# The last stage of a one-core transformer kernel: a written-out pass order, six shared PSUM banks, and the second bias through DRAM

## The chip, the cores and the metric

The kernel runs on one core of a Trainium2 chip. The metric is the device time of one execution in microseconds (us). The core has five engines with a queue of instructions each: PE (TensorE, matmuls), DVE (VectorE), ACT (ScalarE), POOL (GpSimd) and SP (SyncE, which here only starts DMAs). They wait for each other through semaphores. PE writes its results into PSUM, which has eight banks of 128 partitions by 512 fp32 columns; DVE and ACT read them from there.

## The reference

The model is a token embedding, a retention layer, a mixture of experts, a complex retention layer, and a last feed-forward layer whose weights are merged per sequence. Only the last part changes. There are NB = 128 sequences of T = 128 tokens with D = 128 features here, E = 8 task vectors and F = 512 hidden features. `h` is what the earlier parts made, and `x` is its normalised form.

```python
gh = relu(einsum('bsd,hd->bsh', x, gfc1_w) + gfc1_b)
g = (einsum('bsh,eh->bse', gh, gfc2_w) + gfc2_b).mean(axis=1)
W1m = W1 + einsum('be,efd->bfd', g, tv_W1)
b1m = b1 + g @ tv_b1
W2m = W2 + einsum('be,edf->bdf', g, tv_W2)
b2m = b2 + g @ tv_b2
hh = relu(einsum('bsd,bfd->bsf', x, W1m) + b1m[:, None, :])
out = einsum('bsf,bdf->bsd', hh, W2m) + b2m[:, None, :]
res = x + out
h = h + (res - mean(res)) * rsqrt(var(res) + LN_EPS) * lng + lnb
```

So each sequence gets its own two weight matrices, which have to be built (merged) from nine given ones before they are used once.

## The kernel before

`h_all` holds all of `h` in SBUF. The last stage is `merged_phase` (its buffers begin with `d_`). It handles 16 sequences in a pass (`SEQS`), 8 passes (`PASSES`), in groups of four sequences (`GB`, so `PG` = 4 groups a pass). In a pass `q`:

- `merge` on PE builds both weight matrices of 16 sequences at once. A block is one matmul for `SPLIT` = 7 hidden features of all 16 sequences (112 columns); there are 74 blocks for the first matrix and 74 for the second. Four blocks fill a PSUM bank (448 columns): this is a fill. ACT empties the fills of the first matrix into `wm` (`keep`, L2322), DVE those of the second (L2419), 19 fills each, and each has two PSUM banks of its own (`h_bank`).
- For each of the 16 sequences `up` (L2236, four fp32 matmuls, which the profile counts as eight, since fp32 goes in two parts), then `relu` by ACT for half of the hidden features (L2330) and by DVE for the other half (L2427), then `down` (L2252, again four). PE issues up(s) before down(s-1). `up` uses the same four banks as the fills.
- At the first sequence of each group of four PE also puts the second bias into the output bank with a matmul of `ones` by `b2g` (L2248), where `b2g` is the bias rows times `g`, made by POOL (L2138).
- For the next pass, spread over the sequences of this one: DVE takes statistics of `h` (L2383, L2388) and normalises (`x_normalise`, L2394 into `d_xn`), PE turns it (`turn_x`, L2184), ACT copies it into `xT` (L2296), PE makes the gate's hidden values (`gate_hidden`, L2193), ACT sums their relu (L2303), PE and ACT make `g` (`make_g`, L2198, L2309), POOL spreads it into `g_diag` (L2130), which `merge` reads, and PE makes the first bias (`make_b1`, L2203).
- To close a group of four, DVE normalises `h` once more into `res` (`x_restore`, L2394 into `d_res`), adds the output bank (`residual`, L2436), takes statistics (L2440, L2445) and normalises (`r_normalise`, L2455); POOL scales, shifts and adds to `h_all` (`close`, L2147, L2149, L2152); SP stores 256 KB (L2120).

Turned `x` has one bank, gate values have one, outputs have two. The order on each engine is written by hand in `step`. `run_passes` writes the first and the last pass out and runs the six between in a hardware loop, two passes a turn, so the body is executed three times. The waits of `merge`, `up` and `down` are each for at most two counters, `emptied[0]` and `emptied[1]`, one for each evicting engine.

Before the first pass, PE, ACT and DVE prepare `x` and `g` of pass 0 group by group.

The retention stages before it are already written in another style: a `cleared` helper there makes, in the steps that are written out, one wait for every earlier user of a bank (five to seven users; L392), and in the loop a single wait.

## Time and profile before

| | us |
|---|---|
| median of 3 runs (2277.15 to 3790.53) | 2277.54 |
| the profiled execution, device time | 2281.0 |
| its span in the trace | 2278.1 |
| last stage, 1684 to 2278 of the trace | 594 |
| of it: preparation, 1687.0 to first fill at 1713.4 | 26.4 |
| pass 0, first fill to first fill | 68.7 |
| passes 1 to 6 together | 423.7 |
| pass 7 and the end | 72.3 |
| PE busy, whole span | 2023.2 (89%) |
| DVE busy, whole span | 1577.6 (69%) |

The trace's zero is the start of the span. A pass is counted from the first `merge` matmul to the first one of the next pass. In the timeline a row gives the start, the duration, the engine, the line and how many equal instructions follow each other; square brackets tell how long the engine was idle just before and what ended that. PEld is the loading of weights, and PEldq are instructions that PE's sequencer handles alone, such as a wait on a semaphore: they move no data, and the page doesn't count them as busy.

### The profile page before, as it was taken

To read this page: it belongs to the slowest core of one execution; us is meant where nothing else is said; L and a number is where in the kernel's file an instruction comes from. 1 tells how busy PE (TensorE), PEld (TensorE's weight loads), DVE (VectorE), ACT (ScalarE), POOL (GpSimd) and SP (SyncE) were. 2 spreads that over 40 slices of the span, in tenths; PEclk is the share of its full clock that TensorE was granted. 3 is DMA by queue.
4 is the path that set the end of the run, shared out by engine and by line. 5 is a ranking of instruction groups with operands and counts; after the bars stand their busy time and mean duration, and the time that the engine had idled before them with its cause. 6 is when DMAs were issued, how large, how long until landed. Compare 5 with 4: busy or idle time off the path is not lost. (4 is left out here: it accounts for less than half of the span.)

```text
span 2278.1 us, 57687 instructions
## 1 busy us (share of the span) xinstructions
PE 2023.2 (89%) x19468; PEld 1493.1 (66%) x19468; DVE 1577.6 (69%) x4533; ACT 1256.7 (55%) x2588; POOL 1058.1 (46%) x1135
## 2 busy tenths in 40 slices
PE   5989898889868999999994899999978888988897
PEld 2655555555546777777772666666647777777776
DVE  4999999999962222223223799999957777787776
ACT  4766666666632222222223788888845554555553
POOL 4577777777666100000006777877601233222333
PEclk9999999999978999999996999999979999999999
DMA  3122222222115555555552311111100000000000
GB/s 90 49 68 67 67 68 69 65 63 65 54 37 172 159 163 167 162 156 157 164 161 61 124 41 39 38 39 39 33 6 6 15 21 16 15 15 16 20 19 20
DMA packets 97009, 159.76 MB, mean 70 GB/s; under 512 B 19074, under 2 KB 49931, under 8 KB 96756
## 3 DMA queue, kind: packets, MB, share of 16 engines
q1 hardware_dynamic: 66036, 79.53, 12.3%
q0 software_dynamic: 30848, 78.56, 11.4%
q8 instruction: 78, 1.28, 0.2%
q14 instruction: 47, 0.39, 0.1%
HBM read 113.06 MB, written 44.96 MB: 69 GB/s over the span
## 5 line engine op out<-in xcount | busy, mean ns | idle before, releaser
L1292 DVE TENSOR_SCALAR b_hT<-b_hbank,b_w 128x512 f32<-128x512 f32 (+1 forms) x156 | 105.7, 678 | 368.7 <-PE b_hbank L1236 368.6
L344 POOL DMA_INDIRECT sent<-a_xn_mid,a_pos_cur x256 | 253.1, 989 | 81.8 <-issue 81.6
L1466 POOL DMA_INDIRECT c_rows<-done,c_cur_pos x256 | 245.5, 959 | 75.6 <-issue 74.8
L1266 ACT ACTIVATE b_hT<-b_hbank,b_w 128x512 f32<-128x512 f32 (+1 forms) x156 | 98.3, 630 | 322.7 <-PE b_hbank L1236 322.7
L1246 PE MATMUL b_bank<-b_w,b_hT 128*128 128x128 f32 x2160 | 254.2, 275 | 2.1 <-DVE b_hT L1292 2.1
L1246 PEld LDWEIGHTS b_bank<-b_w,b_hT 128*128 128x128 f32 x2160 | 247.5, 192 | 2.4 <-DVE b_hT L1292 2.3
L1236 PE MATMUL b_hbank<-b_xT,b_w 128*128 128x512 f32 (+1 forms) x624 | 246.9, 539 | 1.1 <-DMA b_w<-pack_dram 1.1
L1212 POOL DMA_DIRECT2D done<-b_y x78 | 42.5, 545 | 423.1 <-DVE b_y L1300 405.0
L2219 PE MATMUL d_bank<-d_g_diag,tv 64*128 64x112 f32 x2368 | 167.1, 291 | 34.2 <-DVE d_wm L2419 29.5
L2219 PEld LDWEIGHTS d_bank<-d_g_diag,tv 64*128 64x128 f32 x2368 | 155.0, 199 | 46.6 <-ACT d_wm L2322 34.5
L2419 DVE COPY d_wm<-d_bank 128x448 f32<-128x448 f32 (+1 forms) x152 | 148.5, 1024 | 50.4 <-PE d_bank L2219 48.2
L2322 ACT ACTIVATE d_wm<-d_bank 128x448 f32<-128x448 f32 (+1 forms) x152 | 151.1, 1050 | 56.0 <-PE d_bank L2219 55.7
L1236 PEld LDWEIGHTS b_hbank<-b_xT,b_w 128*128 128x128 f32 x624 | 113.4, 192 | 87.8 <-issue 83.1
L1847 DVE TENSOR_TENSOR c_masked<-c_bank,c_decay 128x512 f32<-128x512 f32 x256 | 162.8, 679 | 6.7 <-PE c_bank L1574 6.5
L745 DVE TENSOR_TENSOR a_masked<-a_scores,a_tabs 128x1024 f32<-128x1024 f32 x128 | 152.8, 1215 | 4.1 <-PE a_scores L475 3.0
L2252 PE MATMUL d_bank<-d_wm,d_hT 128*128 128x128 f32 x1024 | 141.6, 281 | 11.8 <-ACT d_hT L2330 11.1
L2252 PEld LDWEIGHTS d_bank<-d_wm,d_hT 128*128 128x128 f32 x1024 | 124.1, 191 | 40.9 <-ACT d_hT L2330 34.6
L2236 PE MATMUL d_bank<-d_xT,d_wm 128*128 128x128 f32 x1024 | 136.6, 278 | 8.1 <-DVE d_wm L2419 8.1
L331 POOL DMA_INDIRECT a_rows<-table_dram,a_cur_ids x128 | 126.1, 985 | 35.1 <-issue 34.5
L2236 PEld LDWEIGHTS d_bank<-d_xT,d_wm 128*128 128x128 f32 x1024 | 127.6, 194 | 22.1 <-issue 13.4
L2427 DVE TENSOR_SCALAR d_hT<-d_bank,d_b1m 128x128 f32<-128x128 f32 x256 | 77.8, 346 | 78.6 <-PE d_bank L2236 74.4
L2147 POOL TENSOR_TENSOR d_res<-d_res,d_ln_gb 128x512 f32<-128x512 f32 x32 | 40.6, 1269 | 193.0 <-DVE d_res L2455 193.0
(256 smaller groups left out, 4516.5 us busy)
## 6 DMA issues: line engine op xcount, KB each, us to landing
b_w<-pack_dram SPq DMA_DIRECT2D x78, 258.0 KB, 2.7
b_w<-pack_dram SPq DMA_DIRECT2D x78, 256.0 KB, 2.7
b_x<-sent SPq DMA_DIRECT2D x57, 256.0 KB, 2.7
done<-b_y POOLq DMA_DIRECT2D x57, 256.0 KB, 2.4
out_dram<-h_all SPq DMA_DIRECT2D x32, 256.0 KB, 2.3
b_b<-pack_dram SPq DMA_DIRECT2D x78, 64.0 KB, 1.9
tv<-tv_dram SPq DMA_DIRECT2D x1, 4736.0 KB, 15.6
sent<-a_xn_mid,a_pos_cur POOLq DMA_INDIRECT x256
```

Of the source, the lines that this page charges most:

```text
L331: pool.indirect_dma_start(out=rows[:, p, b, :], out_offset=None, in_=table_d, in_offset=bass.IndirectOffsetOnAxis(ap=cur_ids[:, p * GB + b ...
L344: pool.indirect_dma_start(out=sent_d, out_offset=bass.IndirectOffsetOnAxis(ap=pos_cur[:, g.par, b, k:k + 1], axis=0), in_=xn_mid[:, g.par, ...
L745: v.tensor_tensor(masked[:, p, 2 * i:2 * i + 2, :, :, :].rearrange("p r b a t -> p (r b a) t"), score_banks[i][:].rearrange("p r (x t) -> ...
L1236: nc.tensor.matmul(h_bank[c][:, 0:s.rows], w[:, s.par, c * P:(c + 1) * P], xT[:, 0:s.rows], start=True, stop=True).then_inc(h_full, 1)
L1246: m = nc.tensor.matmul(y_bank[s.par][:, j * D:(j + 1) * D], hT[:, c, j * P:(j + 1) * P], w[:, s.par, W2 + c * D:W2 + (c + 1) * D], start=( ...
L1466: pool.indirect_dma_start(out=rows[:, g.par, b, k, :], out_offset=None, in_=done_d, in_offset=bass.IndirectOffsetOnAxis(ap=cur_pos[:, g.pa ...
L1847: v.tensor_tensor(masked[:, p, r, :, :, :, :].rearrange("p i c k t -> p (i c k) t"), score_bank[r][:].rearrange("p (x t) -> p x t", t=L), ...
L2219: m = nc.tensor.matmul(bank_of(q, who, n)[:, at:at + cols], tv[half, k, :], g_diag[half, 0:block_cols(k), :], start=True, stop=True)
L2236: m = nc.tensor.matmul(bank_of(q, who, n)[:, j * T:(j + 1) * T], wm[:, s, 0, c * P:(c + 1) * P], xT[:, q.par, s, :], start=True, stop=True)
L2252: m = nc.tensor.matmul(bank[:, (s % GB) * D:(s % GB + 1) * D], hT[:, s % 2, c, :], wm[:, s, 1, c * D:(c + 1) * D], start=False, stop=(s % ...
L2322: nc.scalar.activation(wm[:, :, 0, at:at + cols].rearrange("p s f -> p f s"), bank_of(q, 0, n)[:, 0:cols * SEQS].rearrange("p (f s) -> p f ...
L2419: v.tensor_copy(wm[:, :, 1, at:at + cols].rearrange("p s f -> p f s"), bank_of(q, 1, n)[:, 0:cols * SEQS].rearrange("p (f s) -> p f s", s= ...
```

## The change

Only the last stage is changed; the lines below are shortened. What it does:

- The passes are written out without a loop: `step` is called for n = -1 to 8, and each call issues work of up to three passes (`p.at(-1)`, `p.at(0)`, `p.at(1)`), in an order that comes from a computed table, a different one on each engine.
- The banks: `work` has six that serve fills, `up`, `turn_x`, `gate_hidden`, `make_g` and the biases alike; two are left for the outputs. Each operation names its bank.
- Fills: both engines now empty a half of each matrix, 20 fills each instead of 19 (18 of four blocks and two small ones).
- PE's waits for a bank: every use on the written-out passes calls `cleared`, which waits for every one of that bank's 12 to 15 users in its latest turn. An operation that takes two banks (a fill, an `up`) waits for the users of both.
- The second bias: PE makes it for 16 sequences with one matmul beside the first bias (`make_biases`), ACT copies it to `b2m`, SP writes it to DRAM (8 KB) and reads it back spread over 128 partitions (256 KB for each group of four), and POOL adds it to `res` (`add_b2`) before `residual`. The four wide bias matmuls of a pass and the four `b2g` multiplications go.
- `x_stats` and `r_stats` have two buffers instead of one.

```diff
-        h_bank, out_bank, turn_bank, gate_bank = (ps[0:2], ps[2:4]), ps[4:6], ps[6], ps[7]
+        work, out_bank = ps[0:6], ps[6:8]
...
-            step(Group(0, 0, 0), "first")
-            with eng.Fori(0, (PASSES - 2) // 2) as j:
-                step(Group(j * 2 + 1, 1, j), "middle")
-                step(Group(j * 2 + 2, 0, j + 1), "middle")
-            step(Group(PASSES - 1, 1, PASSES // 2 - 1), "last")
+            for n in range(-1, PASSES + 1):
+                step(Pass(n, n % 2, n // 2))
...
+            def write_b2(q):
+                sp.wait_ge(g_ready, q.n * 3 + 2)
+                sp.dma_start(b2_rows_d[q.par], b2m[:]).then_inc(b2_written, 16)
+                sp.wait_ge(b2_written, q.n * 16 + 16)
+
+            def spread_b2(q, i):
+                if i >= 2 or q.is_past(1):
+                    sp.wait_ge(b2_added, q.n * PG + (i - 1))
+                sp.dma_start(b2_all[:, i % 2, :, :],
+                             b2_rows_d[q.par, i * GB:(i + 1) * GB, :].partition_broadcast(P)).then_inc(b2_spread[i % 2], 16)
...
+            for n in range(PASSES):
+                q, nxt = (Group(m, m % 2, m // 2) for m in (n, n + 1))
+                spread_b2(q, 2)
+                spread_b2(q, 3)
+                store(q, 0)
+                store(q, 1)
+                if nxt.n < PASSES:
+                    write_b2(nxt)
+                    spread_b2(nxt, 0)
+                    spread_b2(nxt, 1)
+                store(q, 2)
+                store(q, 3)
...
-                pool.tensor_tensor(b2g[:, i % 2, :, :], over(b2_rows.unsqueeze(1), [E + 1, GB, D]),
-                                   over(g[0:E + 1, q.par, i * GB:(i + 1) * GB].unsqueeze(2), [E + 1, GB, D]),
-                                   ALU.mult).then_inc(b2g_ready, 1)
+            def add_b2(q, i):
+                n = q.n * PG + (i + 1)
+                r = res[:, i % 2, :, :]
+                pool.wait_ge(b2_spread[i % 2], q.n * 32 + 16 * (i // 2 + 1))
+                pool.wait_ge(x_again, n)
+                pool.tensor_tensor(r, r, b2_all[:, i % 2, :, :], ALU.add).then_inc(b2_added, 1)
...
+            users0 = ((kept[1], 20, -1, 6), (kept[0], 20, -1, 9), (kept[0], 20, -1, 12), (kept[1], 20, -1, 15), (relued[1], 16, -1, 0), (kept[0], 20, -1, 19), (relued[0], 16, -1, 3), (relued[1], 16, -1, 5), (xT_ready, 4, 0, 1), (relued[1], 16, -1, 9), (xT_ready, 4, 0, 2), (relued[0], 16, -1, 13), (relued[0], 16, -1, 15), (g_ready, 3, 0, 2), (kept[1], 20, 0, 3))
...
+            def cleared(p, users, place):
+                for i, (read, each, off, k) in enumerate(users):
+                    n = min(p.n + off - (i >= place), PASSES - 1)
+                    if n >= 0:
+                        pe.wait_ge(read, n * each + (k + 1))
...
+                    if p.is_edge():
+                        cleared(p, users0, 1)
+                        cleared(p, users3, 1)
+                    else:
+                        pe.wait_ge(kept[1], q.n * 20 + 7)
+                        pe.wait_ge(kept[0], q.n * 20 + 7)
+                    merge(q, 9, (work[0], work[3]))
...
-                    nc.tensor.matmul(bank[:], ones[:], b2g[:, i % 2, :, :], start=True, stop=False)
```

`is_edge()` is true where the pass number is a plain number, which it is in every call here. The tables `users0` to `users5` have 15, 13, 13, 14, 15 and 12 entries. A matmul carries one wait itself; a further wait stands ahead of it in a wait instruction of PE's queue, which holds one or two. So a fill in banks 0 and 3 has 29 waits: one in the matmul and 14 wait instructions. Of PE's queue in the built programs: the last stage before has 253 such instructions for four written passes (0 to 2 ahead of an operation), the last stage now has 4322, which is 307 in pass 0 (86 of them at its fills), 577 to 579 in each of passes 1 to 6 and 536 in pass 7, counted from one `make_g` to the next. Of the 579, 268 stand at the 20 fills, 24 at up 0 and the biases, and 285 from up 1 to up 15.

Where fills follow each other, PE's queue read before (names in brackets are the counters that are waited for; `x7` are the further matmuls of the fill):

```order
L2219 MATMUL d_bank<-d_g_diag,tv 128x112 [waits d_emptied_dve,d_emptied_act]
L2219 MATMUL d_bank<-d_g_diag,tv 128x112 x7
L2219 MATMUL d_bank<-d_g_diag,tv 128x112 [waits d_emptied_dve,d_emptied_act]
L2219 MATMUL d_bank<-d_g_diag,tv 128x112 x7
L2219 MATMUL d_bank<-d_g_diag,tv 128x112 [waits d_emptied_dve,d_emptied_act]
```

The same place now, in the middle of the fills of a pass (each name stands once, however many values of it are waited for):

```order
L2259 MATMUL d_bank<-d_g_diag,tv 128x112 [waits d_kept_act,d_kept_dve,d_relued_dve,d_gh_ready,d_relued_act,d_xT_ready,d_g_ready]
L2259 MATMUL d_bank<-d_g_diag,tv 128x112 x7
L2259 MATMUL d_bank<-d_g_diag,tv 128x112 [waits d_kept_act,d_kept_dve,d_relued_act,d_xT_ready,d_gh_ready,d_relued_dve]
L2259 MATMUL d_bank<-d_g_diag,tv 128x112 x7
L2259 MATMUL d_bank<-d_g_diag,tv 128x112 [waits d_kept_dve,d_kept_act,d_relued_dve,d_g_ready,d_gh_ready,d_relued_act]
```

The matmuls are the same; what grew is the set of waits ahead of each fill.

Where up and down alternate, PE's queue read before, at the start of a pass's sequences:

```order
L2236 MATMUL d_bank<-d_xT,d_wm 128x128 [waits d_emptied_dve,d_emptied_act]
L2236 MATMUL d_bank<-d_xT,d_wm 128x128 x3
L2248 MATMUL d_bank<-d_b2g,d_ones 128x512 [waits d_b2g_ready]
L2252 MATMUL d_bank<-d_wm,d_hT 128x128 [waits d_emptied_dve,d_emptied_act]
L2252 MATMUL d_bank<-d_wm,d_hT 128x128 x3
L2236 MATMUL d_bank<-d_xT,d_wm 128x128 [waits d_emptied_dve,d_emptied_act]
```

and reads now:

```order
L2268 MATMUL d_bank<-d_xT,d_wm 128x128 [waits d_kept_dve,d_kept_act,d_relued_dve,d_xT_ready,d_relued_act,d_gh_ready]
L2268 MATMUL d_bank<-d_xT,d_wm 128x128 x3
L2282 MATMUL d_bank<-d_wm,d_hT 128x128 [waits d_relued_act,d_res_ready,d_relued_dve,d_kept_dve,d_kept_act]
L2282 MATMUL d_bank<-d_wm,d_hT 128x128 x3
L2268 MATMUL d_bank<-d_xT,d_wm 128x128 [waits d_kept_act,d_kept_dve,d_g_ready,d_relued_act,d_xT_ready,d_relued_dve,d_gh_ready]
```

The wide bias matmul (L2248) is gone from this place, `down` waits for its relus as before, and each `up` has the long set of waits. On DVE, after the fills of a pass, the work now reads:

```order
L2872 RECIPROCAL d_r_rstd<-d_r_std 128x4
L2876 TENSOR_SCALAR d_res<-d_res,d_r_mv,d_r_rstd 128x128 x4
L2854 TENSOR_TENSOR d_res<-d_bank6,d_res 128x512
L2845 TENSOR_SCALAR d_hT<-d_bank0,d_b1m 128x128 x2
L2814 RECIPROCAL d_x_rstd<-d_x_std 128x4
L2806 TENSOR_SCALAR d_xn<-h_all,d_x_mv,d_x_rstd 128x128 x4
```

where it read before, at the same normalisation of an output:

```order
L2451 RECIPROCAL d_r_rstd<-d_r_std 128x4
L2455 TENSOR_SCALAR d_res<-d_res,d_r_mv,d_r_rstd 128x128 x4
L2427 TENSOR_SCALAR d_hT<-d_bank2,d_b1m 128x128 x2
L2402 RECIPROCAL d_x_rstd<-d_x_std 128x4
L2394 TENSOR_SCALAR d_xn<-h_all,d_x_mv,d_x_rstd 128x128 x4
```

In both, a normalisation of `x` stands a short way behind one of `res`, whose end starts POOL's `close`.

## Rows read from the trace of the kernel before

**Rows 1.** Busy time by stretch: pass 0, passes 1 to 6, pass 7, preparation.
```profile
core 0: us, PE busy (x) PEld busy (x) DVE busy (x) ACT busy (x) POOL busy (x), PEclk, DMA share, GB/s
1713.39:1782.06 68.67, 64.12 (x596) 55.30 (x595) 54.00 (x161) 39.46 (x97) 10.68 (x10) 0.97 0.03 9
1782.06:2205.76 423.70, 374.92 (x3565) 327.95 (x3564) 330.26 (x1050) 229.43 (x582) 117.91 (x102) 0.98 0.06 17
2205.76:2278.10 72.34, 54.41 (x561) 48.62 (x560) 47.74 (x138) 29.71 (x56) 26.85 (x22) 0.95 0.08 23
1687.00:1713.39 26.39, 15.59 (x37) 8.01 (x37) 9.90 (x52) 9.48 (x42) 1.69 (x3) 0.50 0.02 3
```

**Rows 2.** Timeline of PE in pass 7: its fills, first sequences.
```profile
2205.76 2.04 PE L2219 MATMUL d_bank<-d_g_diag,tv 64*128 64x112 f32 x32
2208.23 2.12 PE L2219 MATMUL d_bank<-d_g_diag,tv 64*128 64x112 f32 x32 [0.42 <-DVE d_wm L2419]
2211.57 2.17 PE L2219 MATMUL d_bank<-d_g_diag,tv 64*128 64x112 f32 x32 [1.22 <-DVE d_wm L2419]
...
2223.29 2.18 PE L2219 MATMUL d_bank<-d_g_diag,tv 64*128 64x112 f32 x32 [0.25 <-DVE d_wm L2419]
2225.73 2.16 PE L2219 MATMUL d_bank<-d_g_diag,tv 64*128 64x112 f32 x32 [0.26 <-DVE d_wm L2419]
...
2230.92 2.02 PE L2236 MATMUL d_bank<-d_xT,d_wm 128*128 128x128 f32 x16 [1.14 <-DVE d_wm L2419]
2232.87 1.12 PE L2248 MATMUL d_bank<-d_b2g,d_ones 9*128 9x512 f32 x2
2233.92 1.16 PE L2252 MATMUL d_bank<-d_wm,d_hT 128*128 128x128 f32 x8
2234.92 1.06 PE L2236 MATMUL d_bank<-d_xT,d_wm 128*128 128x128 f32 x8
2235.81 1.06 PE L2252 MATMUL d_bank<-d_wm,d_hT 128*128 128x128 f32 x8
...
2263.82 2.05 PE L2252 MATMUL d_bank<-d_wm,d_hT 128*128 128x128 f32 x16
```

**Rows 3.** Wait instructions of PE (L392), in three short windows.
```profile
L392 PEldq EVENT_SEMAPHORE  x4: 51/51/51, 94.4 to 94.7; - x4
...
L392 PEldq EVENT_SEMAPHORE  x4: 51/51/51, 115.3 to 115.7; - x4
...
L392 PEldq EVENT_SEMAPHORE  x4: 51/51/51, 627.3 to 627.6; - x4
```

**Rows 4.** Groups by line over passes 1 to 6, DVE's and PE's.
```profile
L2419 DVE COPY d_wm<-d_bank 128x448 f32<-128x448 f32 (+1 forms) x114 | 110.3, 1020 | 32.7 <-PE d_bank L2219 30.9 <-DVE d_r_stats L2440 1.4
L2394 DVE TENSOR_SCALAR d_xn<-h_all,d_x_mv,d_x_rstd 128x128 f32 x96 | 42.6, 507 | 0.9
L2248 PE MATMUL d_bank<-d_b2g,d_ones 9*128 9x512 f32 x48 | 26.9, 640 | 0.0
L2394 DVE TENSOR_SCALAR d_res<-h_all,d_x_mv,d_x_rstd 128x128 f32 x96 | 26.4, 340 | 0.0
```

**Rows 5.** Timeline of a normalisation that meets POOL's work, pass 3.
```profile
1970.50 0.61 DVE L2427 TENSOR_SCALAR d_hT<-d_bank,d_b1m 128x128 f32<-128x128 f32 x2 [0.60 <-PE d_bank L2236]
1971.23 3.91 DVE L2394 TENSOR_SCALAR d_xn<-h_all,d_x_mv,d_x_rstd 128x128 f32 x4
1971.33 1.27 POOL L2149 TENSOR_TENSOR d_res<-d_res,d_ln_gb 128x512 f32<-128x512 f32 x1
1972.79 1.27 POOL L2152 TENSOR_TENSOR h_all<-h_all,d_res 128x512 f32 x1 [0.20 <-POOL d_res L2149]
```

**Rows 6.** Timeline of one up, its two relus and the next up, pass 3.
```profile
1953.76 1.06 PE L2236 MATMUL d_bank<-d_xT,d_wm 128*128 128x128 f32 x8
1954.41 0.63 ACT L2330 ACTIVATE d_hT<-d_bank,d_b1m 128x128 f32<-128x128 f32 x2 [0.74 <-PE d_bank L2236]
1954.86 0.61 DVE L2427 TENSOR_SCALAR d_hT<-d_bank,d_b1m 128x128 f32<-128x128 f32 x2 [1.52 <-PE d_bank L2236]
```

**Rows 7.** PE at a turn of the loop: timeline, and clock by stretch.
```profile
2062.01 1.16 PE L2252 MATMUL d_bank<-d_wm,d_hT 128*128 128x128 f32 x8
2065.34 4.56 PE L2219 MATMUL d_bank<-d_g_diag,tv 64*128 64x112 f32 x48 [2.17 <-issue]
...
1923.00:1930.00 7.00, 6.72 (x64) 6.56 (x64) 4.10 (x8) 3.40 (x4) 4.19 (x4) 0.56 0.15 41
2206.00:2214.00 8.00, 6.09 (x96) 5.62 (x95) 6.57 (x16) 5.57 (x7) 5.65 (x5) 1.00 0.13 36
```

**Rows 8.** Timeline of PE in the preparation of pass 0.
```profile
1692.68 1.08 PE L2184 MATMUL d_bank<-d_ident,d_xn 128*128 128x128 f32 x4 [2.20 <-DVE d_xn L2394]
1694.45 2.07 PE L2193 MATMUL d_bank<-d_xT,d_gfc 128*128 128x512 f32 x2 [0.69 <-ACT d_xT L2296]
1696.32 1.06 PE L2184 MATMUL d_bank<-d_ident,d_xn 128*128 128x128 f32 x4
```

**Rows 9.** DMA issues on the page: the stores of the last stage.
```profile
out_dram<-h_all SPq DMA_DIRECT2D x32, 256.0 KB, 2.3
```

More of the change, by code:

```diff
@@ L46 @@
 BLOCKS = -(-FF // SPLIT)
+SHARE = BLOCKS // 2
 EPS = 1e-5
@@ L2154, in step @@
-            def step(q, place):
-                nxt = None if place == "last" else q.after()
-                b2_by_g(q, 2)
-                close(q, 0)
-                b2_by_g(q, 3)
-                close(q, 1)
-                if nxt:
-                    spread_g(nxt)
-                close(q, 2)
-                if nxt:
-                    b2_by_g(nxt, 0)
-                    b2_by_g(nxt, 1)
-                close(q, 3)
+                pool.wait_ge(norm_step, n * 2)
+                pool.tensor_tensor(r, r, over(ln_gb[:, 0, :].unsqueeze(1), [P, GB, D]), ALU.mult).then_inc(close_step, 1)
@@ L2224, in up, with merge @@
-            def up(q, s):
-                n = FILLS + s
-                for who in range(2):
-                    pe.wait_ge(emptied[who], q.n * USES + (n - 1))
-                if s == 0:
-                    pe.wait_ge(emptied[0], q.n * USES + FILLS)
-                    pe.wait_ge(emptied[1], q.n * USES + FILLS)
+                m = nc.tensor.matmul(bank[0:SEQS, P:P + D], g[0:E + 1, q.par, :], b2_rows, start=True, stop=True)
+                m.then_inc(g_made, 1)
+            def merge(q, k, banks):
+                if k == 0:
+                    pe.wait_ge(g_diag_ready, q.n + 1)
+                fills = [fill_of(k, who) for who in range(2)]
+                last = len(fills[0][1]) - 1
+                for j in range(last + 1):
+                    for who in range(2):
+                        _, blocks, cols, _ = fills[who]
+                        at, n = sum(cols[:j]) * SEQS, cols[j] * SEQS
+                        half = slice(who * HALF, (who + 1) * HALF)
+                        m = nc.tensor.matmul(banks[who][:, at:at + n], tv[half, blocks[j], :],
+                                             g_diag[half, 0:cols[j], :], start=True, stop=True)
+                        if j == last:
+                            m.then_inc(filled[who], 1)
@@ L2233, in up @@
+            def up(q, s, banks):
                 for who in range(2):
@@ L2285, in _ @@
+            pe.wait_ge(loaded, 16 * LOADS)
+            pe.wait_ge(consts, 1)
+            nc.tensor.matmul(work[0][:, 0:2 * D], coef[:], ln_rows, start=True, stop=True).then_inc(ln_step, 1)
+            pe.wait_ge(ln_step, 2)
             pe.wait_ge(tv_loaded, 16)
@@ new lines, in keep @@
+            def keep(q, k, bank):
+                act.wait_ge(filled[0], q.n * FILLS + (k + 1))
+                if k == 0 and q.is_past(1):
+                    act.wait_ge(up_full[1], q.n * SEQS)
+                if k == HALF_FILLS and q.is_past(1):
+                    act.wait_ge(down_done, q.n * SEQS)
+                half, _, cols, at = fill_of(k, 0)
+                n = sum(cols)
+                nc.scalar.activation(wm[:, :, half, at:at + n].rearrange("p s f -> p f s"),
+                                     bank[:, 0:n * SEQS].rearrange("p (f s) -> p f s", s=SEQS),
+                                     ACT.Copy).then_inc(kept[0], 1)
@@ L2423, in relu, with keep @@
-            def relu(q, s):
-                n = FILLS + s
-                dve.wait_ge(full[1], q.n * USES + (n + 1))
+            def keep(q, k, bank):
+                dve.wait_ge(filled[1], q.n * FILLS + (k + 1))
+                if k == 0 and q.is_past(1):
+                    dve.wait_ge(up_full[1], q.n * SEQS)
+                if k == HALF_FILLS and q.is_past(1):
+                    dve.wait_ge(down_done, q.n * SEQS)
+                half, _, cols, at = fill_of(k, 1)
+                n = sum(cols)
+                v.tensor_copy(wm[:, :, half, at:at + n].rearrange("p s f -> p f s"),
+                              bank[:, 0:n * SEQS].rearrange("p (f s) -> p f s", s=SEQS)).then_inc(kept[1], 1)
```

921 lines of the change are left out of this document (678 added, 243 removed).

## The prediction

> **What bounds the kernel now.** Only the last stage changes, so I read it alone: first the busy time by stretch, then PE's timeline inside a pass, then the groups by line. A pass of the steady part takes 423.70/6 = 70.6 us, with PE 62.5 and DVE 55.0 us busy in it [rows 1]. Neither is full. The timeline shows two parts. The fills run from 2205.76 to 2230.92, 25.2 us for 19 on each evicting engine [rows 2]. There PE makes two fills in 2.04 to 2.18 us and then sits 0.25 to 0.42 us until DVE has emptied a bank: 2.42 us for two, where PE needs about 2.04 alone. DVE needs 1.02 us for one copy [rows 4], so also 2.04 for two. Two banks an engine don't let these two overlap fully. The rest, some 45 us, alternates up and down, 0.89 us each (2234.92 to 2235.81), with a wide bias matmul of 1.05 us at every fourth sequence (2232.87 to 2233.92) and the next pass's preparation between them [rows 2]. Its stalls are PE waiting for relus. At the two turns of the loop PE also has nothing in its queue for about 2 us, and runs the next matmuls at a granted clock of 0.56 over 7 us, so partly at 1.2 GHz [rows 7].
>
> **What the array and DVE still have to do in a pass.** PE: 18 full fills at 1.02 and two small, 19.1; 32 ups and downs at 0.89, 28.5; four turns and four gate matmuls about 5.2; g and biases about 1.5. That is 54 us. DVE: the 55.0 of now. If nothing else stood in the way, the computed order and the shared banks could bring a pass to about 60 us.
>
> **The waits.** What speaks against it is PE's queue. In the trace of now four wait instructions in a row start within 0.3, 0.4 and 0.3 us of each other's first, so nine intervals in 1.0 us, 0.11 us each, although each lasts only 51 ns and all have long been satisfied [rows 3]. (They stand in the written-out steps of the first stage.) Read to a tenth, the price lies between 0.10 and 0.12. Now there are 577 to 579 of them in each steady pass: 579 x 0.11 = 63.7 us of PE's sequencer, which can overlap with the array's matmuls already queued but not with itself.
> - Fills: 268 wait instructions for 20 fills, 29.5 us, against 25.2 now. A fill costs 13.4 x 0.11 = 1.47 us of sequencer where its matmuls take 1.02 and its copy 1.02. The sequencer takes over from the banks as the limit. Three rounds of banks are now plenty: a copy has 3 x 1.47 us.
> - The first up (16) and the biases (8): 24 x 0.11 = 2.6 us.
> - Ups and downs, from up 1 to up 15: 285 wait instructions, 31.4 us, and 31 us of array work, nearly equal. One up has 14 waits and its down one, 1.65 us of sequencer. But down(s) waits for both relus of up(s): DVE's ends at 1954.86 + 0.61 = 1955.47, 1.71 us after that up's start [rows 6], and the counter must still arrive, say 1.9. The sequencer stands at that wait and only then begins the next up's 14. So 1.9 us a sequence, 0.25 over its own 1.65: 31.4 + 15 x 0.25 = 35.2.
> - DVE in the same part: 55.0 less 110.3/6 = 18.4 of copies [rows 4], so 36.6. From this about 2.7 us (one output's normalisation, one addition, one aggregate and relu 0) now stand among the fills: 33.9. To it comes a collision. Normalising x takes 507 ns where the same operation into `res` takes 340 [rows 4]; 96 x 0.167/6 = 2.7 us a pass, and one case is visible: four of them take 3.91 us where 1.11 is usual, while POOL works on `res` and `h_all` [rows 5]. In the new order two normalisations of x (groups 1 and 2) follow one of `res` closely, and POOL's `close` begins in between. I take two collisions a pass for one: 33.9 + 2.7 = 36.6, say 37 with the ends. That is a little over PE's 35.2, so it stands.
>
> Steady pass: 29.5 + 2.6 + 37 = 69.1 us, 1.5 less than now, 9 us for six.
>
> **The other passes.** Pass 0 takes 68.7 [rows 1]. Its operations have 307 wait instructions, few in its fills (86), so these go at about 1.1 us (copy and hand-over): 22. Up 0 and biases: 1. DVE has no group of an earlier pass to close, so PE's 35.2 and some unevenness, 36. Together 59, 9 saved. Pass 7: its fills cost 29.5 for 25.2; its four bias matmuls of 1.05 us go; its sequences take (34.95 - 4.2)/16 = 1.92 us now, from 2230.92 to the end of the last down at 2265.87 [rows 2] and 1.9 by the above. So 0, and the tail of normalising and closing is the same chain. Preparation: gate and turn matmuls follow each other within 4.2 us a group now, since one bank each serves them [rows 8]; the new one overlaps groups, but at half clock a group's turn and gate take 3.15 us of PE and the last gate sum stays: 2 saved.
>
> **What is costed at nothing.** The second bias: its matmul is one for 16 sequences, about 0.1 us more. The DRAM write and the 256 KB reads are of the size of the stores, 2.3 us from issue to landing [rows 9]; a chain of two is 5 us, from `make_biases` to the first `add_b2`, between which all fills of the pass lie (29 us). Behind SP's wait for the write stand two stores, for which nothing waits but the two-deep `res`, by way of `close`, not by the store itself. POOL exchanges four multiplications of about 1.03 for four additions of about 1.27 us, 1 us of some 50 free. The loop's end: its empty queue, 2.17 us in one row, is part of the 70.6 that I replace.
>
> The Trainium skill ("Runtime: NRT & Kernel Launch", Instruction fetch mechanics) says that a taken branch breaks sequential prefetch, and that unrolling avoids this stall. The trace agrees: `issue` stands only at the loop's turns. By that rule alone the gain would be some 4 us of empty queue and a little clock.
>
> **The sum.** 9 + 9 + 0 + 2 = 20. The profiled execution took 2281.0, so 2261; the median shown is 3.5 lower, so 2257.5 against 2277.5, rounded to 2258.
>
> **Rivals.**
> 1. The waits are cheap. If satisfied waits on counters long passed cost under 0.07 us, 14 of them hide behind a fill's 1.02 us. For: the matmuls' queue lets the array work meanwhile. Against: the 0.11 of three places. Then DVE bounds: 18.4 + 2.7 + 37 + 2 = 60 us a pass, 6 x 10.6 + 9 + 2 + 4 (pass 7) = 79 us: 2199. Chance 0.13.
> 2. Slower: the clock. A fill then keeps the array busy 1.02 of 1.47 us, 69%. After 2 us without matmuls the granted clock was 0.56 over the next 7, while with PE busy 6.09 of 8 it stayed 1.00 [rows 7]. If the gaps in the fills lower the clock, a fill's matmuls take 2.04 us; over all fills of eight passes that is 160 x 0.57 = 91 us, so 2349. It is slower by over 2% if the clock is down in over 0.7 of the fills. For: 0.45 us gaps in every fill, for 29 us. Against: pass 7 had gaps of 1.22 us and kept its clock. Chance 0.08 for over 2%, the same again for a partial drop (2260 to 2300).
> The Trainium skill ("TensorE: Matmul & The Clock Gate", A second HAM failure mode: psum-queue depth-cycling) tells of short idle times between groups of matmuls that make the clock fall and rise. The 0.56 is the nearest this trace has to it; the sum of rival 2 is its price here.
> 3. The change doesn't shorten the rest because DVE and PE wait for each other in turn, at 72 to 74 us a pass: their orders were computed together, but for durations without the waits' cost. 2270 to 2290, chance 0.2, within 2%.
>
> **Chances and range.** 2% is 45.5 us, about what a measurement of this kernel can tell from no change. Mine 0.51; rival 1 0.13, rival 2 0.16, rival 3 0.20. Own bounds: the wait at 0.10 or 0.12 moves 292 of them a pass by 2.9 us, 20 us over seven; without any collision PE's 35.2 holds, 12 less. So 2226 to 2278. Part of my case at 0.10, and rival 1 in part, reach below 2232. Faster by over 2%: 0.15; within: 0.77; slower: 0.08. Range 2215 to 2300.
>
> **What would show it.** Steady passes of 67 to 71 us; fills about 1.5 us apart with PE idle some 0.45 us before each and the copies waiting for PE, no longer PE for the copies; that idle time put down to `issue`, not to DVE; PE's clock at 1.00 in the fills; pass 0 near 59 us and the first fill by 1711. I am wrong if the fills stand 1.1 us apart (rival 1), if PE's clock falls in them (rival 2), or if DVE waits more than 5 us a pass for ups (rival 3).

## The result and the profile after

The changed kernel takes 2315.1 us (median of four runs, 2312.8 to 2315.9) against 2277.5 for the kernel before beside it: ratio 1.016, 95% interval 1.014 to 1.018. (A fourth execution of the kernel before, at 3790.5 us, was a slow one and isn't counted.) So the change makes the kernel slower by 38 us, where I had forecast 20 us less, and the time lies outside the range. Its profiled execution took 2315.3 us and spans 2313.6 us in the trace.

The busy time by stretch, for the changed kernel: pass 0, passes 1 to 6, pass 7 with the end, and then pass 4 in two parts, from its first fill to the end of its last fill, and from there to the next pass.

```profile
core 0: us, PE busy (x) PEld busy (x) DVE busy (x) ACT busy (x) POOL busy (x), PEclk, DMA share, GB/s
1709.57:1773.61 64.04, 59.01 (x572) 54.80 (x573) 51.43 (x156) 37.51 (x97) 11.80 (x10) 0.90 0.09 27
1773.61:2231.44 457.83, 377.77 (x3528) 335.27 (x3529) 353.95 (x1047) 237.69 (x595) 124.45 (x103) 0.95 0.10 29
2231.44:2313.60 82.16, 58.90 (x578) 54.06 (x578) 52.24 (x145) 31.40 (x60) 28.98 (x23) 0.91 0.12 33
2001.74:2036.31 34.57, 28.03 (x330) 25.09 (x330) 22.02 (x33) 20.54 (x25) 4.96 (x4) 0.90 0.08 25
2036.31:2077.84 41.53, 35.43 (x259) 31.55 (x259) 37.16 (x146) 18.95 (x77) 15.79 (x14) 0.96 0.11 33
```

Beside [rows 1]: pass 0 went from 68.7 to 64.0 us, but a steady pass from 70.6 to 457.83/6 = 76.3, and pass 7 with the end from 72.3 to 82.2. PE's busy time hardly moved (374.92 and 377.77 in six passes). That hides a rise, for the wide bias matmuls, 26.9 us of it before [rows 4], are gone; the granted clock is 0.95 instead of 0.98, and a fill that stands alone counts 1.15 us where two in a row count 2.04. PE's sequencer, the part that works through its queue, has more to do. These are the wait instructions of `cleared` (L2226) in passes 1 to 6, and, below the "...", those ahead of one single fill. The columns are the count, the duration of one in ns (least, median, most) and the first and last start.

```profile
L2226 PEldq EVENT_SEMAPHORE  x3270: 51/51/411, 1773.8 to 2231.2; - x193
...
L2226 PEldq EVENT_SEMAPHORE  x13: 51/51/51, 2009.9 to 2011.2; - x13
```

Thirteen of them fill the 1.3 us between the starts of the first and the last: 0.108 each, as in [rows 3]. Fills now look like this (PE's timeline, pass 4; compare [rows 2], where pairs of fills stand 2.44 us apart and wait for DVE):

```profile
2003.33 1.15 PE L2259 MATMUL d_bank<-d_g_diag,tv 64*128 64x112 f32 x16 [0.44 <-issue]
2004.40 1.06 PE L2243 MATMUL d_bank<-d_g,d_rows 9*128 9x16 f32 x8
2005.39 0.39 PE L2245 MATMUL d_bank<-d_rows,d_g 9*16 9x128 f32 x2
2005.71 1.16 PE L2282 MATMUL d_bank<-d_wm,d_hT 128*128 128x128 f32 x8
2006.80 1.15 PE L2259 MATMUL d_bank<-d_g_diag,tv 64*128 64x112 f32 x16
2008.35 1.15 PE L2259 MATMUL d_bank<-d_g_diag,tv 64*128 64x112 f32 x16 [0.40 <-issue]
2009.84 1.15 PE L2259 MATMUL d_bank<-d_g_diag,tv 64*128 64x112 f32 x16 [0.34 <-issue]
2011.31 1.15 PE L2259 MATMUL d_bank<-d_g_diag,tv 64*128 64x112 f32 x16 [0.32 <-issue]
```

The fills stand 1.47 to 1.55 us apart, the array idles 0.3 to 0.4 us ahead of each, and the idle time is put down to `issue`. The groups on the page agree: the copies wait for PE (92.7 and 87.8 us), PE for the copies hardly at all.

```profile
L2259 PE MATMUL d_bank<-d_g_diag,tv 64*128 64x112 f32 (+1 forms) x2368 | 181.2, 298 | 49.2 <-issue 31.5
L2835 DVE COPY d_wm<-d_bank 128x448 f32<-128x448 f32 (+1 forms) x160 | 153.2, 984 | 92.7 <-PE d_bank L2259 92.3
L2685 ACT ACTIVATE d_wm<-d_bank 128x448 f32<-128x448 f32 (+1 forms) x160 | 157.4, 1013 | 87.8 <-PE d_bank L2259 87.3
```

The other part of the pass is where I was more wrong. These rows are from DVE's, POOL's and PE's timelines of that part, in this order, out of the same 19 us of pass 4; the last row shows PE's wait instructions just ahead of the last matmul row:

```profile
2045.44 1.11 DVE L2876 TENSOR_SCALAR d_res<-d_res,d_r_mv,d_r_rstd 128x128 f32<-128x128 f32 x4
2047.79 3.17 DVE L2806 TENSOR_SCALAR d_xn<-h_all,d_x_mv,d_x_rstd 128x128 f32<-128x128 f32 x4
2050.89 0.60 DVE L2845 TENSOR_SCALAR d_hT<-d_bank,d_b1m 128x128 f32<-128x128 f32 x2
2055.87 1.12 DVE L2876 TENSOR_SCALAR d_res<-d_res,d_r_mv,d_r_rstd 128x128 f32<-128x128 f32 x4
2057.11 4.26 DVE L2806 TENSOR_SCALAR d_xn<-h_all,d_x_mv,d_x_rstd 128x128 f32<-128x128 f32 x4
2061.58 0.57 DVE L2845 TENSOR_SCALAR d_hT<-d_bank,d_b1m 128x128 f32<-128x128 f32 x2
...
2057.06 1.27 POOL L2182 TENSOR_TENSOR d_res<-d_res,d_ln_gb 128x512 f32<-128x512 f32 x1 [1.18 <-DVE d_res L2876]
2058.41 1.27 POOL L2184 TENSOR_TENSOR d_res<-d_res,d_ln_gb 128x512 f32<-128x512 f32 x1
2059.76 1.27 POOL L2187 TENSOR_TENSOR h_all<-h_all,d_res 128x512 f32<-128x512 f32 x1
...
2051.63 1.13 PE L2282 MATMUL d_bank<-d_wm,d_hT 128*128 128x128 f32 x8 [1.08 <-DVE d_hT L2845]
2062.93 0.63 PE L2231 MATMUL d_bank<-d_ident,d_xn 128*128 128x128 f32 x4 [1.91 <-ACT d_hT L2696]
...
L2226 PEldq EVENT_SEMAPHORE  x6: 51/51/51, 2062.2 to 2062.7; - x6
```

Twice in this stretch a normalisation of x, 1.11 us when undisturbed, takes 3.17 and 4.26 us and ends 0.3 us after POOL's three operations of `close` (in the second case 2057.11 + 4.26 = 2061.37, and 2059.76 + 1.27 = 2061.03). The relu behind it is late, and PE stands just there. In the first case it stands at `down`, 1.08 us, until DVE's relu ends at 2051.49. In the second it stands 1.91 us ahead of `turn_x`, which first waits for the users of its bank. The profile puts this down to ACT's relu, but of the wait instructions in the view above, six start from 2062.2 on, just behind the end of DVE's relu (2061.58 + 0.57 = 2062.15), and the matmul follows them at 2062.93. So PE's queue stood at the wait for DVE's relu, and worked through the other waits of the same bank only afterwards. A third case (the normalisation of `res` at 2068.68, 2.14 us, beside POOL's `add_b2`) makes 6.2 us of collisions in the pass.

### The profile page after: what moved, and what is told of

It is laid out like the page before. It is cut to its first block and busy times, and to the rows that moved or that the text cites. A ratio compares the mean times of both kernels' runs of the same rounds, so it can differ in the third digit from the quotient of the medians.

```text
span 2313.6 us, 60759 instructions
## 1 busy us (share of the span) xinstructions
PE 2027.6 (88%) x19420; PEld 1506.4 (65%) x19420; DVE 1602.5 (69%) x4541; ACT 1266.9 (55%) x2604; POOL 1065.6 (46%) x1134
## 5 line engine op out<-in xcount | busy, mean ns | idle before, releaser
L2259 PE MATMUL d_bank<-d_g_diag,tv 64*128 64x112 f32 (+1 forms) x2368 | 181.2, 298 | 49.2 <-issue 31.5
L2835 DVE COPY d_wm<-d_bank 128x448 f32<-128x448 f32 (+1 forms) x160 | 153.2, 984 | 92.7 <-PE d_bank L2259 92.3
L2259 PEld LDWEIGHTS d_bank<-d_g_diag,tv 64*128 64x128 f32 x2368 | 161.5, 204 | 69.1 <-issue 53.6
L2685 ACT ACTIVATE d_wm<-d_bank 128x448 f32<-128x448 f32 (+1 forms) x160 | 157.4, 1013 | 87.8 <-PE d_bank L2259 87.3
L2175 POOL TENSOR_TENSOR d_res<-d_res,d_b_all 128x512 f32<-128x512 f32 x32 | 40.6, 1270 | 337.6 <-DVE d_res L2806 337.6
L2268 PE MATMUL d_bank<-d_xT,d_wm 128*128 128x128 f32 x1024 | 148.5, 293 | 26.2 <-issue 10.2
L2268 PEld LDWEIGHTS d_bank<-d_xT,d_wm 128*128 128x128 f32 x1024 | 132.8, 203 | 45.3 <-issue 36.5
L2696 ACT ACTIVATE d_hT<-d_bank,d_b1m 128x128 f32<-128x128 f32 x256 | 80.2, 366 | 113.8 <-PE d_bank L2282 77.5
L2282 PEld LDWEIGHTS d_bank<-d_wm,d_hT 128*128 128x128 f32 x1024 | 130.6, 199 | 16.9 <-issue 8.9
```

The source lines that it names most:

```text
L2259: m = nc.tensor.matmul(banks[who][:, at:at + n], tv[half, blocks[j], :], g_diag[half, 0:cols[j], :], start=True, stop=True)
L2268: m = nc.tensor.matmul(banks[who][:, j * T:(j + 1) * T], wm[:, s, 0, c * P:(c + 1) * P], xT[:, q.par, s, :], start=True, stop=True)
L2282: m = nc.tensor.matmul(bank[:, (s % GB) * D:(s % GB + 1) * D], hT[:, s % AHEAD, c, :], wm[:, s, 1, c * D:(c + 1) * D], start=(c == 0), sto ...
L2685: nc.scalar.activation(wm[:, :, half, at:at + n].rearrange("p s f -> p f s"), bank[:, 0:n * SEQS].rearrange("p (f s) -> p f s", s=SEQS), A ...
L2835: v.tensor_copy(wm[:, :, half, at:at + n].rearrange("p s f -> p f s"), bank[:, 0:n * SEQS].rearrange("p (f s) -> p f s", s=SEQS)).then_inc ...
```

## The experiments

Theory A: the wait instructions set the pass. B: DVE's and PE's orders make them wait for each other in turn whatever the waits cost. C: the half clock costs the time. Two more came up after the first runs. By D, what the collisions take is added to PE's time; by E, it is hidden beside it. Medians stand against 2277.0, 2277.6 and 2274.1 for the kernel before in the three sets, and against 2315.1 for the changed one, which ran apart from them. "A pass" is the mean of passes 1 to 6.

### Short waits on PE

PE's queue runs in order, so a condition that an earlier wait of it implies needn't be asked again.

```diff
+            known = {}
+            def need(sem, n):
+                if known.get(id(sem), 0) < n:
+                    pe.wait_ge(sem, n)
+                    known[id(sem)] = n
...
-                        pe.wait_ge(read, n * each + (k + 1))
+                        need(read, n * each + (k + 1))
```

> The changed kernel, but PE's queue leaves out each condition that an earlier wait of the same queue already implies (the same semaphore for the same or a higher count). A steady pass holds 31 wait instructions on PE instead of 579; order, banks and the bias through DRAM are unchanged. Theory A (PE's sequencer, at 0.106 us for each wait instruction, sets the pass): fills 1.05 us apart instead of 1.5, steady passes near 61 us instead of 76.3, DVE the bound, about 2210 us in all. Theory B (DVE and PE wait for each other in turn because of the computed order; the waits mostly lie beside work): the pass stays above 72 us, about 2285. Theory C (the half clock costs the time, and it comes from the order): clock still down once or twice a pass, 2290 or more.

Measured: 2191.7 us, ratio to the kernel before 0.963 (0.960 to 0.965), 123 us below the changed kernel. Passes 1 to 6 and the two parts of pass 4; then all that is left of its wait instructions in those six passes (31 a pass instead of 579):

```profile
1764.23:2121.79 357.56, 331.70 (x3530) 309.18 (x3529) 339.48 (x1045) 223.91 (x596) 124.10 (x102) 0.99 0.13 37
1943.67:1966.18 22.51, 22.30 (x332) 21.14 (x331) 20.01 (x35) 18.39 (x27) 5.10 (x4) 1.00 0.13 37
1966.18:2002.80 36.62, 32.47 (x259) 29.73 (x259) 35.87 (x136) 18.92 (x75) 15.54 (x13) 1.00 0.12 30
...
L2217 PEldq EVENT_SEMAPHORE  x186: 51/51/51, 1766.6 to 2121.6; - x186
```

A pass takes 59.6 us; the time is even 18 us under the 2210 that theory A gave. Theory A stands, B falls: the order, the banks and the path of the bias are those of the changed kernel. The fills' part went from 34.6 to 22.5 us, with the array busy for 22.3 of it; the other from 41.5 to 36.6, with DVE busy for 35.9.

### Which waits, and how many

One condition for each semaphore and bank, the highest (232 wait instructions a pass):

```diff
-                        pe.wait_ge(read, n * each + (k + 1))
+                        last[id(read)] = max(last.get(id(read), (read, 0)), (read, n * each + (k + 1)), key=lambda w: w[1])
+                for read, value in last.values():
+                    pe.wait_ge(read, value)
```

> The changed kernel with one condition for each semaphore and bank, the highest count: 232 wait instructions on PE in a steady pass instead of 579, 5 a fill (0.53 us of sequencer) and 5 an up. Theory A with a threshold (waits are free as long as a group's waits take less than the array's 1.02 or 0.89 us for that group): within 12 us of the kernel with 31 waits a pass, so about 2220. If instead each wait adds its time wherever it stands: 347 of 548 removed, so two thirds of the way, about 2247. Theory B or C: 2285 or more.

Measured: 2203.1 us, a pass of 61.5. Of the 548 wait instructions in question the first 201 cost 1.9 us a pass and the other 347 cost 14.8. The price isn't proportional: five a fill (0.53 us) lie nearly hidden beside the array's work (the fills' part of pass 4 takes 23.4 us, with 31 waits a pass 22.5), 13 (1.4 us) don't.

Short waits ahead of the fills alone, and everywhere but there (`need` in place of `pe.wait_ge` in the calls concerned):

> The changed kernel with the short waits only ahead of the fills (16 wait instructions for 20 fills instead of 268); the other groups keep theirs (321 in a steady pass). Theory A: fills 1.05 us apart, 8 to 9 us less a pass, the part of ups and downs as in the changed kernel; about 2250. If DVE's and PE's turn-taking in the ups sets the time: about the same, since the fills are outside it. If the full waits of the fills only hide what the copies would cost: 2300. The clock should stay at 1.00 in the fills.

> The changed kernel with the short waits everywhere but ahead of the fills (fills keep 268 wait instructions, 286 in a steady pass). Theory A: fills 1.5 us apart as in the changed kernel, the ups and downs 5 to 7 us shorter a pass; about 2265. If the ups' waits lie hidden beside the relus of ACT and DVE: about 2310. The two partial kernels should together give nearly what the kernel with all waits short gives, if the two parts of a pass add.

Measured: 2222.1 and 2266.7 us. Pass 4 in its two parts, first with short waits in the fills, then with short waits in the rest:

```profile
1959.27:1982.81 23.54, 22.29 (x331) 21.01 (x330) 20.01 (x34) 18.70 (x27) 5.11 (x4) 1.00 0.12 36
1982.81:2022.96 40.15, 34.09 (x259) 30.00 (x259) 37.32 (x144) 19.14 (x75) 15.58 (x13) 1.00 0.13 34
...
1977.63:2010.71 33.08, 27.08 (x332) 24.03 (x331) 22.73 (x35) 20.79 (x26) 5.09 (x4) 0.95 0.09 26
2010.71:2047.14 36.43, 32.27 (x259) 29.66 (x259) 35.31 (x136) 18.57 (x75) 15.56 (x13) 1.00 0.13 30
```

Each part answers to its own waits: 10.6 to 11.0 us in the fills, 3.5 to 5.1 in the rest. I had expected 28 us too little from the fills (2250 for 2222); the rest came within 2 us. The two savings, 93 and 48 us, come to 18 more than the 123 of both at once. They don't simply add, and why isn't shown.

### The same waits in the kernel before

```diff
+                    for _ in range(MORE):
+                        pe.wait_ge(g_diag_ready, q.n + 1)
+                        pe.wait_ge(consts, 2)
                     for j, k in enumerate(blocks_of(n)):
```

Each turn of this small loop adds two conditions, and one wait instruction carries both, so `MORE` is the number of wait instructions added.

> The kernel before with 12 more wait instructions ahead of each fill's matmuls (13 in place of 1), all on counters that were reached long ago. If each costs PE's sequencer 0.106 us whatever the kernel: a fill takes 13 x 0.106 and the hand-over, about 1.49 us instead of 1.25, 4.5 us a pass, 36 in all: 2313. If satisfied waits are hidden beside the array's queue: 2277. If waits against a register (inside the loop) cost more than against a constant, the middle passes grow by more than pass 7.

> The kernel before with 6 more wait instructions ahead of each fill (7 in place of 1). With 12 more a fill took 1.58 us and the kernel 41 us more. If waits are free as long as the sequencer's time of a fill (7 x 0.106 + 0.15 = 0.9 us) is under what the banks and copies allow (1.25 us): 2277 to 2283. If each wait costs its time: 2298.

Measured: with 12 more 2318.7 us (ratio 1.018, 1.016 to 1.020), with 6 more 2278.2 (1.0015, 1.0000 to 1.003). The kernel before becomes as slow as the changed one by these waits alone, and with seven ahead of a fill it loses 4 us by the medians, 0.15%, which is at the edge of what can be told from nothing. PE's timeline with 12 more, in pass 7:

```profile
2241.16 1.15 PE L2224 MATMUL d_bank<-d_g_diag,tv 64*128 64x112 f32 x16 [0.29 <-issue]
2242.65 1.15 PE L2224 MATMUL d_bank<-d_g_diag,tv 64*128 64x112 f32 x16 [0.34 <-issue]
```

That is 1.49 us from fill to fill for 13 wait instructions: 13 x 0.106 and 0.11 more. I call these 0.11 us the hand-over from a group's waits to its matmuls; the trace gives the remainder and not its cause. The other fills of this pass stand up to 1.8 us apart.

### The clock

```diff
+                            for _ in range(AGAIN[who] if last == 3 else 0):
+                                m = nc.tensor.matmul(banks[who][:, at:at + n], tv[half, blocks[j], :],
+                                                     g_diag[half, 0:cols[j], :], start=True, stop=True)
                             m.then_inc(filled[who], 1)
```

> The changed kernel with all its waits; each full fill issues its last block's matmul three times more (twice in one half of the array's rows, once in the other) into the same place with the same values, so that the array has some 1.4 us of work in each 1.49 us of a fill instead of 1.02. Nothing else changes. If the waits alone set the pass (theory A), the extra matmuls stand beside the sequencer's waits: 2315 within 6 us, with the half-clock stretches gone from the fills. If the half clock costs time of its own (theory C, 8.0 us a steady pass at half clock in the changed kernel against 1.7 with short waits), removing it gives back up to 0.5 us for each of some 3 fills a pass: 1.5 us a pass, so 2303. If a matmul instruction costs the sequencer as much as a wait: 3 x 0.106 x 18 a pass more, 2350 or more.

Measured: 2330.0 us, 15 more, which is none of the three times expected (2315, 2303, 2350). Pass 0 and passes 1 to 6:

```profile
1709.70:1783.90 74.20, 69.81 (x680) 66.12 (x681) 53.72 (x157) 39.54 (x98) 11.94 (x11) 0.86 0.08 23
1783.90:2246.80 462.90, 413.80 (x4178) 377.18 (x4178) 357.93 (x1046) 241.95 (x595) 124.14 (x103) 0.98 0.10 29
```

The granted clock over passes 1 to 6 rose from 0.95 to 0.98, and the pass still took 77.2 us instead of 76.3. Ten of the 15 us fall in pass 0 (74.2 for 64.0), whose fills have few waits, so that the added matmuls find no gap there. This alone doesn't settle theory C, for the added work may hide a gain.

The passes of one kernel say more, since passes 1 to 6 run the same instructions, at clocks that differ. These are pass 3 and pass 6 of the changed kernel and pass 3 without its fills; below the "...", passes 2 and 3 of the kernel with short waits:

```profile
1926.91:2001.74 74.83, 60.04 (x588) 52.63 (x589) 59.27 (x177) 39.62 (x101) 20.71 (x18) 1.00 0.11 30
2154.56:2231.44 76.88, 64.47 (x588) 57.95 (x589) 57.27 (x166) 39.56 (x100) 20.74 (x18) 0.91 0.11 29
1961.27:2001.74 40.47, 34.01 (x259) 30.10 (x259) 37.18 (x145) 18.97 (x77) 15.76 (x14) 1.00 0.12 34
...
1824.40:1883.40 59.00, 54.62 (x592) 50.80 (x590) 55.93 (x171) 37.47 (x101) 20.67 (x17) 1.00 0.12 33
1883.40:1943.70 60.30, 56.02 (x591) 52.30 (x590) 57.78 (x184) 37.34 (x100) 20.71 (x17) 0.97 0.15 41
```

Pass 3 of the changed kernel had the full clock throughout and took 74.8 us; the other five, at 0.91 to 0.96, took 76.1 to 76.9. The fills hardly share in this (34.4 us in pass 3, 34.3 to 34.9 in the others); the ups and downs do, with 40.5 against 41.5 to 42.4. So I put about 1.5 us a pass on the mean down to the lower clock in the changed kernel, some 9 us over the six. (It rests on one pass; with short waits the same comparison gives 1.3 us.) At full clock in both, a pass still takes 74.8 us with all waits and 59.0 with short ones. In the kernel with added matmuls the passes at full clock took 76.1 and 76.0 us: the added work itself costs 1.2 and hid the gain. The clock is a small part of the loss, the waits are the large one.

### The collisions

Three moves in DVE's order take the normalisations away from POOL's work: `x_normalise(q, 1)` behind `relu(q, 7)`, `r_normalise(q, 0)` behind `x_normalise(q, 2)` and `x_mean_var(q, 3)`, `r_normalise(q, 1)` behind `relu(q, 12)`. The second as a diff:

```diff
-                    r_normalise(q, 0)
-                if q := p.at(0):
+                if q := p.at(0):
                     dve.wait_ge(x_stats_ready, q.n * PG + 4)
                     x_normalise(q, 2)
                     x_mean_var(q, 3)
                 if q := p.at(-1):
+                    r_normalise(q, 0)
                     relu(q, 9, work[0])
```

> The changed kernel with all its waits; only DVE's order differs: the normalisations of x of groups 1 and 2 no longer stand behind a normalisation of the residual, whose end starts GpSimd's three operations of close, and the one of group 1's residual comes later than the restoring of group 2. In the changed kernel those three take 3.17, 4.26 and 2.14 us in a pass where 1.11 is usual, 6.2 us more, while GpSimd works, and PE stands 2.98 and 3.21 us for DVE's relus behind the first two. Theory D (what the collisions take is added to PE's own time, since PE's queue stands at down's wait meanwhile and catches nothing up): 4 to 6 us less a pass, 2272 to 2290. Theory E (the waits alone make the ups and downs 41.8 us; the collisions lie beside them): 2315.

> The kernel with short waits and the same three moves in DVE's order. DVE bounds that kernel (56 to 58 us busy of 59.6), so the 6.2 us of collisions should come off: 4 to 5.5 us a pass where PE's 55 us become the bound, 2150 to 2165. If GpSimd's close only collides with whatever DVE does next: within 8 us of 2192.

Measured: 2289.4 with all waits (26 less), 2171.3 with short ones (20 less; ratio to the kernel before 0.954, 0.952 to 0.956, the fastest of all). The kernel before ran 3 us faster in this set, so against it the savings are 22 and 18 us. The first time lies in the 2272 to 2290 of theory D; the second is above the 2150 to 2165 that I had expected. The later part of pass 4 in each:

```profile
2021.01:2059.56 38.55, 35.37 (x258) 31.41 (x259) 31.80 (x145) 18.72 (x77) 15.73 (x14) 0.96 0.13 36
```

```profile
1959.16:1992.97 33.81, 32.56 (x260) 29.63 (x259) 31.62 (x142) 19.62 (x77) 15.65 (x13) 1.00 0.12 32
```

With the 41.53 and 36.62 above this is a table of four: the waits cost 4.9 us with the collisions and 4.7 without, the collisions cost 3.0 with the waits and 2.8 without. The clock is alike in each pair that gives the collisions' cost (0.96 and 0.96, 1.00 and 1.00). The waits' cost here holds some of the clock's: between passes at full clock (40.47 above, and 36.62) it is nearer to 4. Neither covers the other, as theory D has it. PE's waits over passes 1 to 6 of the changed kernel show the same 3 us (us in total, times, longest):

```profile
PE d_bank L2231 <- ACT d_hT L2696: 11.7, 6, 2.1
PE d_bank L2282 <- DVE d_hT L2845: 6.3, 6, 1.1
```

These are the two stands above, 18.0 us or 3.0 a pass, and with DVE's order changed both are gone. The collisions themselves were expected to give more: the normalisations of x and `res` became shorter by 16 x (665 - 384) + 16 x (406 - 347) ns = 5.4 us a pass, as the next rows show, and a little over half of that came off.

DVE's groups over passes 1 to 6 of the changed kernel, and of the same with DVE's order changed:

```profile
L2806 DVE TENSOR_SCALAR d_xn<-h_all,d_x_mv,d_x_rstd 128x128 f32<-128x128 f32 x96 | 57.9, 665 | 1.1 <-DVE d_x_rstd L2814 0.3
L2876 DVE TENSOR_SCALAR d_res<-d_res,d_r_mv,d_r_rstd 128x128 f32<-128x128 f32 x96 | 33.0, 406 | 1.0
```

```profile
L2806 DVE TENSOR_SCALAR d_xn<-h_all,d_x_mv,d_x_rstd 128x128 f32<-128x128 f32 x96 | 30.8, 384 | 0.9
L2876 DVE TENSOR_SCALAR d_res<-d_res,d_r_mv,d_r_rstd 128x128 f32<-128x128 f32 x96 | 27.3, 347 | 1.0
```

In the fastest kernel PE is busy for 32.56 of the 33.81 us: the array is the bound at last. The relus and residuals, which read PSUM and now stand beside `close`, aren't slowed: with DVE's order changed a relu takes 344 ns and a residual 678, in the changed kernel 343 and 678. The Trainium skill ("SBUF — State Buffer", SBUF: two separate sides) calls the pair of ports that DVE and GpSimd share "an exclusive lock, not a bandwidth split", held for a whole instruction, and names the kinds of DVE operation that need it. The 4.26 us agree with that: the normalisation grew by 3.15 us beside three POOL operations, which kept their 1.27 us each.

### The second bias and the loop

The kernel with short waits, with the bias by a wide matmul as in the kernel before. In the first form GpSimd's product for a group stood behind `close` of an earlier one; the second form puts it ahead.

```diff
-                pool.tensor_tensor(r, r, b2_all[:, i % 2, :, :], ALU.add).then_inc(b2_added, 1)
+                pool.tensor_tensor(b2g[:, i % 2, :, :], over(b2_rows.unsqueeze(1), [E + 1, GB, D]),
+                                   over(g[0:E + 1, q.par, i * GB:(i + 1) * GB].unsqueeze(2), [E + 1, GB, D]),
+                                   ALU.mult).then_inc(b2_added, 1)
...
+                    need(b2_added, q.n * PG + (i + 1))
+                    nc.tensor.matmul(bank[:], ones[:], b2g[:, i % 2, :, :], start=True, stop=False)
```

> The kernel with short waits, but the second bias as in the kernel before: GpSimd multiplies the bias rows by g, a wide matmul starts each group's bank, nothing goes through DRAM and GpSimd adds nothing to the residual. PE gets about 4 us a steady pass more. If DVE bounds the pass with short waits (its work about 55 us of 59.6), most of that hides: 2192 to 2205. If PE bounds it, 4 us a pass more: 2220. If the detour through DRAM delays the residuals, the matmul is faster: under 2185.

> The kernel with short waits and the second bias by a matmul, with GpSimd's multiplications of the bias rows ahead of the close of two groups back, so that PE doesn't wait for them. In the first form of this kernel PE stood 49.7 us in 5.8 passes for a multiplication that stood behind close. If that order was the whole of its 99 us: 2192 to 2215, PE's 4 us a pass for the wide matmuls being the rest. If the wide matmul itself costs the time: 2270 or more.

Measured: 2290.4 and 2224.2 us, both outside what I had expected of them (up to 2220, and 2192 to 2215 or over 2270). Most of the first one's 99 us was my own edit, as PE's waits from 1790 to 2200 us show (us in total, times, longest):

```profile
PE d_bank L2284 <- POOL d_b2g L2169: 49.7, 12, 5.0
```

The wide matmul stood there for a product that POOL made only behind `close`. The second form still has 32.5 us more than 2191.7, 4.1 us a pass (382.10/6 = 63.7, with PE busy for 60.4), about the 4.2 that PE's four wide matmuls of 1.05 take. DVE being the fuller engine didn't hide them. So the way through DRAM is worth 4 us a pass here, and its own cost isn't seen; no run takes it away alone.

The kernel before with the passes written out, `with eng.Fori(...)` replaced by `for j in range(...)`:

> The kernel before with its six middle passes written out instead of three turns of a loop; nothing else. The empty queue of some 2 us at each turn goes, and the half clock behind it: passes after a turn 69.5 instead of 71.8. About 7 us in all, 2270. If the loop explained a large part of what the short-wait kernel gains (85 us), it would be 2255 or less; if it costs nothing, 2277.

Measured: 2270.8 us, ratio 0.998 (0.9965 to 0.9994): 7 us by the medians, as expected. The Trainium skill's rule that a taken branch breaks the prefetch of instructions ("Runtime: NRT & Kernel Launch", Instruction fetch mechanics) agrees with this in direction; the size is these 7 us, and no run tells the prefetch from anything else that the loop's turn costs.

## Why the prediction was wrong

- **Base, preparation, pass 0.** The first fill starts at 1709.6, 4 us earlier (2 forecast). Pass 0 took 64.0 us, not 59; with short waits it took 61. Its fills made most of that, 26.2 us where I had put 22, at a granted clock of 0.82; with short waits they took 25.2 at 0.81. I had no term for the clock there.
- **The price of a wait instruction, 0.11 us.** Right. Thirteen in 1.4 us in the changed kernel, and the kernel before slows by 41 us with 12 more a fill, where the expectation at this price was 36.
- **The fills, 29.5 + 2.6 = 32.1 us.** Right in kind (spacing, idle time, `issue`, copies waiting), too low by 2.5: 34.57 in pass 4. (The pair of fills that I read as 2.42 us apart stands 2.44 apart in [rows 2]; nothing hangs on it.) The hand-over was missing: 0.11 us a fill. And the biases went in by their waits alone, though their matmuls and a `down` occupy the array: 3.47 us between two fills (2003.33 to 2006.80), where 8 + 14 + 1 waits would make 2.4.
- **Ups and downs, 37 us as the larger of DVE's 36.6 and PE's 35.2.** This step failed: with the waits the part takes 41.5 in pass 4 and 41.8 on the mean of six. DVE's figure was right; with short waits the part took 36.2 to 37.9. Taking the larger of the two assumes that DVE's excess lies beside PE's work. But PE's queue stands at the wait for a relu while a collision holds DVE back, and it can't use that time for the wait instructions behind this one. So what the collisions hold up adds to PE's time, 3.0 us. PE's own 35.2 was too low as well: without most of the collisions the part takes 38.55. Of the 3.3 us between, the clock accounts for 1 to 2, by an estimate from pass 3 against the others; I had held it at 1.00. The rest isn't shown; 30 hand-overs of 0.11 us would be enough for it, but it wasn't tried. The collisions' places, groups 1 and 2, were right, and their size nearly: I had counted 5.4 us (2.7 that were in DVE's 55.0 already and 2.7 on top) where there were 6.2.
- **Pass 7: 0.** It took 9.8 us more. The stretch from its first fill to the end of its last, 34.5 us (row below), is as long as in the other passes; I had put 29.5 for it from the fills' waits alone, but `up` 0 with its waits stands in it, and the hand-overs. What follows it took 47.7 us (2265.91 to 2313.6) where the kernel before takes 47.2 from its first `up` on [rows 2]: the four wide matmuls saved are eaten up by the waits (with short waits it takes 43.1).

```profile
2231.44:2265.91 34.47, 27.22 (x330) 24.02 (x330) 21.79 (x29) 20.44 (x24) 4.90 (x4) 0.95 0.09 25
```

- **The miss.** 6 x (76.3 - 69.1) = 43 in the steady passes, 5 in pass 0, 10 in pass 7, less 2 in the preparation: 56 us. The forecast's 2261 and the 2315.3 of the profiled execution are 54 apart.
- **Rivals.** Rival 3 (in turn, 72 to 74 us a pass) had the mechanism nearest to it, at less than the 76.3 measured. Its sign, DVE waiting more than 5 us a pass for ups, was met with 32.6/6 = 5.4, but it says little, as the kernel before has 56.3/6 = 9.4 ahead of the same relus. Rival 1's 2199 is what the kernel would take if the waits were free: 2191.7 was measured with 31 a pass. Rival 2, the clock: it did fall, to 0.95 over the steady passes, against my sign of 1.00 in the fills, and cost about 1.5 us a pass, in the ups and downs rather than in the fills where the rival had put it.
